# Two orders of their own in the first attention: one for its first step, one for its last

## The chip, the cores and the metric

The kernel runs on one core of a Trainium2 chip. Its engines work side by side and wait for each other through semaphores: TensorE (matmuls), VectorE, ScalarE (called ACT in the profile), GpSimd (POOL) and SyncE (SP), whose queue starts the DMAs here. The metric is the device time of one execution in microseconds (us). The kernel before took 1471.29 us, the median of three runs (1468.84 to 1474.14).

## The reference: what is computed

Two pre-norm transformer layers on `x` of 2 batches x 1024 tokens x 128 channels, in float32. Only the first attention matters here:

```python
q = z @ wq @ fcq_w + fcq_b          # z = layernorm(x); 16 heads of 64
k = z @ wk @ fck_w + fck_b
v = z @ wv @ fcv_w + fcv_b
scores = jnp.einsum('bihd,bjhd->bhij', q, k) / scale
attn = jax.nn.softmax(scores, axis=-1)
out = jnp.einsum('bhij,bjhd->bihd', attn, v)
x = x + (out.reshape(b, n, 1024) @ fco_w + fco_b)
```

It is followed by a mixture of 8 experts with the best 2 chosen per token (its router: a softmax over 8 logits, the two largest, their places), a second attention and a second mixture.

## The kernel before, in words

`l0_attention` works in 16 steps (`STEPS0`): for each of the 2 batches 8 pairs of heads. One step handles 1024 queries against 1024 keys for two heads, in 16 score tiles: 8 blocks of 128 keys (`kt`) times 2 halves of 512 queries (`j`). Softmax needs an upper bound of each row first, so every step also prepares the step behind it.

A step is a list of words (`STEP`), which `step_script` turns into units; every engine runs through the same list and takes its own part of each unit, so the list is the order on every engine:

- `ST`: a score tile. TensorE makes four matmuls into one of three buffers (L933, L934), ACT writes the exponential into `prob` (L680). GpSimd adds the tiles of the eight key blocks for the row sums, two adds of 128x1024 for each block (L623, L628). In the last step GpSimd adds for one head and VectorE for the other (`add_last`, L790).
- `PV`: the product of the probabilities with the values (L906), four matmuls, two units behind the scores (`VALUES_BEHIND`).
- `q`: projections of the next step. TensorE L854, then ACT L638, then VectorE L733.
- `s`: scores of the next step, used for their maxima alone. TensorE L863 and L865, VectorE reduces a tile (L739). There are 16.
- `m`: the maxima turned into a row. TensorE L884, VectorE L744 and L747, then a DMA (`max_rows`, L528) puts the row where the next step's scores read it (`pe.wait_ge(row_loaded, ...)` ahead of `ST` 0).
- `l`: row sums of the step before (TensorE L890, VectorE L751, DMA L536). `r`: their inverse (VectorE L771), sent out and broadcast by DMAs (L541, L544). `n`: the scaling of the output by it (VectorE L775). `g`: output product (TensorE L895, VectorE L779). `r` and `n` have no TensorE part; `g` on TensorE waits for `n`.
- `R`, `X`, `P`: parts of the router for the first batch, in steps 12 and 14, not touched.

`ST`, `q`, `s`, `m`, `l` and `g` share the ring of three score buffers in PSUM (`RING`): a unit may write only when the unit three places before it in the list has been read. An exponential of block `kt` also waits for the value product and the sums of block `kt - 4`, because `prob` has four buffers.

Step 0 has no step behind it whose sums, inverse, scaling and output are due, so `l`, `r`, `n`, `g` and its first two `PV` drop out of the list. The last step has no step to prepare; its list is `LAST_STEP`, and VectorE also does the router's choice for the first batch in it: `probabilities` and `choose_two` after the first sum (L1007 to L1016), when ACT has made the router's exponential (`EXP_AT`, L710), and `index_two` (L1023 to L1029) after the second. Behind the last step stand two value products, the last row sums and the end of the stage.

Of the kernel before, what the change touches and what calls it, by code (L numbers as in the profile page):

```python
# [19 lines left out]
TT = T // P  # L20
# [11 lines left out]
STEPS0 = B * PAIRS  # L32
# [336 lines left out]
def step_units(k_next, k_done):  # L369

    return ([("q", 0), ("q", 1)] * k_next
            + [("s", x) for x in range(S_UNITS)] * k_next + [("m", 0)] * k_next
            + [("l", 0), ("r", 0), ("n", 0), ("g", 0)] * k_done)


STEP = ("ST ST ST ST q q ST PV PV s s s PV PV s s PV ST ST l s s PV X r PV s s s PV PV ST ST ST ST "
        "n ST ST PV s s PV PV s s s PV PV PV s ST ST m g R P PV ST ").split()
LAST_STEP = ("ST ST ST ST PV PV PV PV ST ST ST ST l PV PV PV PV ST ST ST ST PV PV r PV PV ST ST ST ST n "
             "PV PV PV PV g ").split()
VALUES_BEHIND = 2  # L380
TURN_AT, ROOT_AT, NORMAL_AT, LEAD_AT, EXP_AT = 6, 12, (4, 6), 12, 4


STATISTICS_BEHIND = (3, 8)
# [4 lines left out]
def step_script(n):  # L389

    has = step_units(n + 1 < STEPS0, n > 0) + EARLY.get(n, [])
    at = defaultdict(int, PV=-VALUES_BEHIND)
    out = []
    for kind in STEP if n + 1 < STEPS0 else LAST_STEP:
        x = at[kind]
        at[kind] += 1
        if kind in ("ST", "PV"):
            if x >= 0 or n:
                out.append((kind, x // 2, x % 2))
        elif (kind, x) in has:  # L400
            out.append(("UNIT", kind, x))
    return out
# [9 lines left out]
def step_order(n):  # L412

    return [u[1:] for u in step_script(n) if u[0] == "UNIT"]
# [17 lines left out]
def ring_of_pairs():  # L432

    tiles = [("UNIT", u) for u in range(len(in_psum(FIRST_UNITS)))]
    for n in range(STEPS0):
        for what, *rest in step_script(n):
            if what == "ST":
                tiles.append(("ST", 2 * TT * n + 2 * rest[0] + rest[1]))
            elif what == "UNIT" and rest[0] not in "rn":
                tiles.append(("UNIT", place(n, tuple(rest))))  # L440
    return tiles + [("UNIT", first_of(STEPS0))]
# [6 lines left out]
def l0_attention(nc, m, d):  # L448
    with ExitStack() as ctx:
# [182 lines left out]
        def _(act):  # L632
# [24 lines left out]
            for u, (kind, x) in enumerate(in_psum(FIRST_UNITS)):  # L657
                if kind == "q":
                    project(0, x, u)
            for n in range(STEPS0):  # L660
                for what, *rest in step_script(n):
                    if what == "UNIT":
                        if rest[0] == "q":
# [52 lines left out]
        def _(v):  # L716
# [65 lines left out]
            def add_last(kt):  # L782

                v.wait_ge(exp_done, 2 * TT * LAST + 2 * kt + 1 + 1)
                total = psum_k[LAST % 2][:, 1, :]
                if kt == 1:
                    v.wait_ge(filled, place(LAST - 1, ("l", 0)) + 1)
                else:
                    v.wait_ge(last_summed, kt - 1)
                nc.vector.tensor_tensor(total, prob[0][:, 1, :] if kt == 1 else total, prob[kt % 4][:, 1, :],  # L790
                                        ALU.add).then_inc(last_summed, 1)
# [38 lines left out]
            for what, *rest in step_script(LAST):  # L830
                if what == "UNIT":
                    unit(*rest, seen, LAST - 1)
                    seen += rest[0] not in "rn"
                elif what == "ST" and rest[1] and rest[0]:
                    add_last(rest[0])
                    if rest[0] == 1:
                        v.wait_ge(early_act, EXP)
                        probabilities(nc, m, link)
                        choose_two(nc, m, link)
                    if rest[0] == 2:  # L840
                        index_two(nc, m, link)
            run(LAST_UNITS, first_of(STEPS0), LAST, None)

# [160 lines left out]
def probabilities(nc, m, link):  # L1004

    shape = [P, HALF, NEXP]
    link(nc.vector.reduce_sum(m.col[:, 1, :], m.ex[:, :, :], AX.X))  # L1007
    link(nc.vector.reciprocal(m.col[:, 2, :], m.col[:, 1, :]))
    link(nc.vector.tensor_tensor(m.probs[:, :, :], m.ex[:, :, :], m.col[:, 2, :].unsqueeze(2).to_broadcast(shape),
                                 ALU.mult))  # L1010


def choose_two(nc, m, link):

    for t in range(HALF):
        ins = nc.vector.max(m.top[:, t, :], m.probs[:, t, :])  # L1016
    link(ins)


def index_two(nc, m, link):  # L1020

    for t in range(HALF):
        ins = nc.vector.max_index(m.idx[:, t, :], m.top[:, t, :], m.probs[:, t, :])  # L1023
    link(ins)
    nc.vector.tensor_copy(m.idxf[:, :, :], m.idx[:, :, 0:TOPK])
    link(nc.vector.tensor_tensor(m.col[:, 3, :], m.top[:, :, 0], m.top[:, :, 1], ALU.add))
    link(nc.vector.reciprocal(m.col[:, 4, :], m.col[:, 3, :]))
    nc.vector.tensor_tensor(m.col[:, 5, :], m.top[:, :, 0], m.col[:, 4, :], ALU.mult)
    link(nc.vector.tensor_tensor(m.col[:, 6, :], m.top[:, :, 1], m.col[:, 4, :], ALU.mult))  # L1029
# [1693 lines left out]
```

## Time and profile before

| | |
|---|---|
| runs | 1474.14, 1468.84, 1471.29 us |
| profiled execution: own time | 1475.02 us |
| profiled execution: span, first to last instruction | 1473.3 us |
| mean granted TensorE clock | 0.965 |
| first attention, scores of step 0 to the end of its last row sums | 64.8 to 736 us |
| busy VectorE, ACT, GpSimd | 974.1, 810.0, 870.9 us |

The page of the profile gives one execution. A row of its grouped parts is a line of the kernel, the engine, the operation, what it writes and reads, the count, the busy time and the mean duration, and then how long the engine stood idle before these instructions and who ended the idle time. A busy TensorE is not TensorE at its peak: at a granted clock of 0.5 the same matmul takes twice as long and is still busy.

### The profile page before, as it was taken

Reading aid. Unit: us, or ns where it says so; the run is one execution under the profiler, and the core shown is the slowest. Engines: PE = TensorE matmul, PEld = TensorE weight load, DVE = VectorE, ACT = ScalarE, POOL = GpSimd, SP = SyncE. Lnnn points to the kernel's source line nnn. Section 1 sums busy time; section 2 is a strip of 40 time slices with the busy share of each in tenths; the row PEclk is TensorE's granted clock in tenths of the full one; section 3 lists DMA queues with packets and bytes.
Section 4 is the critical chain, followed back from the end, with each engine's and each line's share of the span. In section 5 each row is a group of like instructions: output and inputs, shape, how many; then the busy total and the mean of one; then the engine's idle time right before and its main releaser. Section 6 shows DMA issues by size and latency. Waiting matters only on the chain. (4 is left out here: it accounts for less than half of the span.)

```text
span 1473.3 us, 18699 instructions
## 1 busy us (share of the span) xinstructions
PE 1367.5 (93%) x6354; PEld 791.1 (54%) x6354; DVE 974.1 (66%) x1675; ACT 810.0 (55%) x1236; POOL 870.9 (59%) x685
## 2 busy tenths in 40 slices
PE   7699999999999999999888876999999988999998
PEld 5345555455544555455366633454445446687776
DVE  5676767767776766666556568677666624566665
ACT  4234454454444454354354452566776666787776
POOL 0277888988888888878544405555655232344443
PEclk9699999999999999999999898999999997999999
DMA  3101111111101111000050006011111107000000
GB/s 107 33 1 59 59 59 59 44 59 59 46 28 59 58 59 45 1 16 27 15 160 1 1 1 100 16 30 30 30 22 24 30 1 273 1 1 8 8 8 8
DMA packets 32586, 60.59 MB, mean 41 GB/s; under 512 B 9499, under 2 KB 17084, under 8 KB 32348
## 3 DMA queue, kind: packets, MB, share of 16 engines
q1 hardware_dynamic: 32492, 59.40, 14.6%
q8 instruction: 51, 0.84, 0.2%
q14 instruction: 43, 0.35, 0.1%
HBM read 35.13 MB, written 13.89 MB: 33 GB/s over the span
## 5 line engine op out<-in xcount | busy, mean ns | idle before, releaser
L628 POOL TENSOR_TENSOR psum_k<-psum_k,prob 128x1024 f32<-128x1024 f32 x186 | 466.6, 2541 | 115.4 <-ACT prob L680 114.9
L680 ACT ACTIVATE prob<-pair 128x1024 f32<-128x1024 f32 x256 | 247.7, 1027 | 367.1 <-PE pair L934 366.9
L739 DVE TENSOR_REDUCE mx<-pair 128x2 f32<-128x1024 f32 x256 | 297.2, 1214 | 40.4 <-PE pair L865 38.5
L906 PE MATMUL pv<-prob,c_all 128*64 128x512 f32 x1024 | 251.0, 607 | 0.9 <-ACT plain L648 0.9
L1937 DVE CUSTOM_DVE_ANT_0 l_banks<-l_banks,causal 128x128 f32<-128x128 f32 (+7 forms) x256 | 189.4, 782 | 75.5 <-PE l_banks L1975 74.4
L1845 ACT ACTIVATE l_prob<-l_banks 128x1024 f32<-128x1024 f32 (+7 forms) x256 | 155.2, 654 | 111.7 <-PE l_banks L1994 111.1
L933 PE MATMUL pair<-qq,ak 128*128 128x512 f32 x512 | 210.9, 412 | 6.0 <-issue 2.8
L934 PE MATMUL pair<-q,kb 128*128 128x512 f32 x512 | 203.5, 397 | 0.0
L2153 POOL TENSOR_TENSOR silu_rest_t<-silu_t,silu_lead_t 128x512 fp32r<-128x512 f32 x74 | 96.3, 1303 | 145.9 <-ACT silu_lead_t L2350 145.9
L1899 POOL TENSOR_SCALAR_AFFINE_SELECT l_prob<-l_prob 128x128 f32<-128x128 f32 x256 | 72.3, 295 | 146.7 <-ACT l_prob L1845 145.1
L933 PEld LDWEIGHTS pair<-qq,ak 128*128 128x128 f32 x512 | 97.7, 191 | 70.4 <-issue 29.2
L2519 DVE TENSOR_TENSOR silu_t<-silu_t,bank_t 128x512 f32<-128x512 f32 x128 | 87.9, 688 | 64.4 <-ACT silu_t L2341 60.4
L1975 PE MATMUL l_banks<-l_kk,l_qq 128*128 128x512 f32 (+3 forms) x384 | 114.4, 391 | 14.7 <-DMA l_qq<-rounded 5.2
L906 PEld LDWEIGHTS pv<-prob,c_all 128*64 128x64 f32 x1024 | 61.1, 136 | 119.2 <-issue 110.4
L2341 ACT ACTIVATE silu_t<-bank_t,b_t 128x512 f32<-128x512 f32 x144 | 99.3, 690 | 43.5 <-PE bank_t L953 43.4
L1994 PE MATMUL l_banks<-l_qq,l_kk 128*128 128x512 f32 (+3 forms) x384 | 111.9, 384 | 4.3 <-DVE plain L1937 3.3
L934 PEld LDWEIGHTS pair<-q,kb 128*128 128x128 f32 x512 | 97.8, 191 | 19.3
L863 PE MATMUL pair<-ak,qq 64*128 64x512 f32 x256 | 97.8, 463 | 8.3 <-DVE mx L739 5.3
L1975 PEld LDWEIGHTS l_banks<-l_kk,l_qq 128*128 128x128 f32 x384 | 64.6, 198 | 73.8 <-ACT l_prob L1845 23.5
L863 PEld LDWEIGHTS pair<-ak,qq 64*128 64x128 f32 x256 | 43.7, 189 | 108.0 <-DVE mx L739 40.6
L865 PE MATMUL pair<-kb,qq 64*128 64x512 f32 x256 | 98.0, 463 | 0.0
L1994 PEld LDWEIGHTS l_banks<-l_qq,l_kk 128*128 128x128 f32 x384 | 62.6, 194 | 54.0 <-issue 21.5
(318 smaller groups left out, 2283.0 us busy)
## 6 DMA issues: line engine op xcount, KB each, us to landing
plain<-scratch_sums SPq DMA_DIRECT2D x32, 256.0 KB
whole<-in_experts SPq DMA_DIRECT2D x12, 512.0 KB, 5.0
scratch_lead<-rounded SPq DMA_DIRECT2D x12, 512.0 KB, 2.6
scratch_rest<-rounded SPq DMA_DIRECT2D x12, 512.0 KB, 3.9
w_lead_t<-scratch_lead SPq DMA_DIRECT2D x9, 512.0 KB, 6.4
w_rest_t<-scratch_rest SPq DMA_DIRECT2D x9, 512.0 KB, 7.3
l_kk<-rounded SPq DMA_DIRECT2D x16, 256.0 KB, 4.2
l_qq<-rounded SPq DMA_DIRECT2D x16, 256.0 KB, 5.3
```

The source lines that it names most:

```text
L628: nc.gpsimd.tensor_tensor(total[:, h, :], total[:, h, :], prob[kt % 4][:, h, :], ALU.add).then_inc(summed, 1)
L680: nc.scalar.activation(prob[kt % 4][:, :, ts(j, BLK)], buffer("ST", at)[:, :, :], ACT.Exp, scale=D0 ** -0.5).then_inc(exp_done, 1)
L739: nc.vector.reduce_max(mx[:, x % 2, :, x // 2], buf[:, :, :], AX.X).then_inc(read, 1)
L863: nc.tensor.matmul(buf[:, 0, :], qq[k % 2][0][0:D0, ts(t, P)], m.ak[0:D0, keys], start=True, stop=True)
L906: ins = nc.tensor.matmul(pv[D0 * h:D0 * (h + 1), ts(j, BLK)], m.c_all[:, TT * (s // PAIRS) + kt, :], prob[kt % 4][:, h, ts(j, BLK)], start ...
L933: nc.tensor.matmul(buf, m.ak[:, keys], qq[n % 2][h][:, ts(j, BLK)], start=True, stop=False)
L934: ins = nc.tensor.matmul(buf, m.kb[:, keys], q2[n % 2][:, h, ts(j, BLK)], start=False, stop=True)
L1845: nc.scalar.activation(prob[kt % 2][:, g, P * kt:T], buffer(item)[:, P * kt - T:], ACT.Exp, scale=SCALE1).then_inc(exp_done, 1)
L1937: ins = nc.vector.tensor_tensor_reduce(scores[:, 0:s_width(t)], scores[:, 0:s_width(t)], hidden, 1.0, -3e38, ALU.add, ALU.max, mx[:, g, t: ...
L1975: ins = nc.tensor.matmul(out[:, lo:end], qq[k % 2][:, g, ts(t, P)], kk[k % 2][:, g, lo:end], start=True, stop=True)
L1994: ins = nc.tensor.matmul(buf[:, at:at + end - lo], kk[n % 2][:, g, ts(kt, P)], qq[n % 2][:, g, lo:end], start=True, stop=True)
L2341: nc.scalar.activation(s[n % R][:, :], bank_of(n)[:, :], ACT.Silu, bias=b1[:, c:c + 1]).then_inc(silu_done, 1)
```

## The change

Step 0 gets a list of its own, `FIRST_STEP`, with the same units: `q q` come first, then five `ST`; seven `ST` stand in a row in the middle; after `m` come two `ST` and two `PV`, where one `PV` and one `ST` stood. In `LAST_STEP`, `r` moves from behind `ST` 11 and four `PV` to between `ST` 10 and `ST` 11, `n` from behind `ST` 15 to ahead of `ST` 12, and two `PV` move from ahead of `ST` 12 to behind `ST` 15. ACT makes the router's exponential after score tile 3 instead of 4. `index_two` moves from behind the sum of block 2 to behind the sum of block 7.

```diff
@@ -375,10 +375,12 @@
 STEP = ("ST ST ST ST q q ST PV PV s s s PV PV s s PV ST ST l s s PV X r PV s s s PV PV ST ST ST ST "
         "n ST ST PV s s PV PV s s s PV PV PV s ST ST m g R P PV ST ").split()
-LAST_STEP = ("ST ST ST ST PV PV PV PV ST ST ST ST l PV PV PV PV ST ST ST ST PV PV r PV PV ST ST ST ST n "
+FIRST_STEP = ("PV PV q q ST ST ST ST ST s s PV s s PV PV s s PV ST ST ST ST ST ST ST s PV s s s PV PV PV "
+              "s s s PV PV s s PV PV s s ST ST m ST ST PV PV ").split()
+LAST_STEP = ("ST ST ST ST PV PV PV PV ST ST ST ST l PV PV PV PV ST ST ST r ST PV PV n ST ST ST ST PV PV "
              "PV PV PV PV g ").split()
 VALUES_BEHIND = 2
-TURN_AT, ROOT_AT, NORMAL_AT, LEAD_AT, EXP_AT = 6, 12, (4, 6), 12, 4
+TURN_AT, ROOT_AT, NORMAL_AT, LEAD_AT, EXP_AT = 6, 12, (4, 6), 12, 3
@@ -391,7 +393,7 @@
-    for kind in STEP if n + 1 < STEPS0 else LAST_STEP:
+    for kind in FIRST_STEP if n == 0 else STEP if n + 1 < STEPS0 else LAST_STEP:
@@ -837,7 +839,7 @@
-                    if rest[0] == 2:
+                    if rest[0] == TT - 1:
                         index_two(nc, m, link)
```

## Rows read from the trace of the kernel before

**Rows 1.** Page, busy time, share of the span and instructions of each engine.

```profile
PE 1367.5 (93%) x6354; PEld 791.1 (54%) x6354; DVE 974.1 (66%) x1675; ACT 810.0 (55%) x1236; POOL 870.9 (59%) x685
```

**Rows 2.** Page, costliest groups: adds on GpSimd, exponentials, maxima.

```profile
L628 POOL TENSOR_TENSOR psum_k<-psum_k,prob 128x1024 f32<-128x1024 f32 x186 | 466.6, 2541 | 115.4 <-ACT prob L680 114.9
L680 ACT ACTIVATE prob<-pair 128x1024 f32<-128x1024 f32 x256 | 247.7, 1027 | 367.1 <-PE pair L934 366.9
L739 DVE TENSOR_REDUCE mx<-pair 128x2 f32<-128x1024 f32 x256 | 297.2, 1214 | 40.4 <-PE pair L865 38.5
```

**Rows 3.** Stretches (start:end, length, busy us by engine, clock): step 0, step 2.

```profile
64.83:107.51 42.68, 39.57 (x165) 21.32 (x165) 25.22 (x24) 18.89 (x22) 26.95 (x12) 0.93 0.05 13
149.36:190.50 41.14, 41.14 (x186) 20.82 (x184) 29.95 (x29) 19.44 (x24) 34.66 (x15) 1.00 0.16 53
```

**Rows 4.** Timeline, TensorE, around step 0's start: start, duration, [idle before].

```profile
61.00 1.01 PE L884 MATMUL pair<-ident,mx 128*16 128x128 f32 x4 [2.69 <-DVE mx L739]
64.83 0.77 PE L933 MATMUL pair<-qq,ak 128*128 128x512 f32 x1 [2.82 <-issue]
...
71.29 2.01 PE L854 MATMUL pair<-aq,w_all 128*128 128x512 f32 x8
73.14 0.40 PE L933 MATMUL pair<-qq,ak 128*128 128x512 f32 x1
```

**Rows 5.** Timeline, DMA queue, the row of maxima.

```profile
62.88 0.61 SPq L528 DMA_DIRECT2D q<-mrow  x1
```

**Rows 6.** Stretches at the lower clock: step 0, step 1, last step.

```profile
64.80:70.50 5.70, 5.67 (x13) 4.47 (x14) 0.00 (x0) 2.22 (x3) 0.00 (x0) 0.50 0.32 92
...
108.10:111.30 3.20, 3.20 (x9) 2.48 (x8) 1.60 (x1) 1.58 (x2) 3.20 (x2) 0.52 0.24 96
...
729.00:732.40 3.40, 3.36 (x6) 1.05 (x8) 0.00 (x0) 0.00 (x0) 0.00 (x0) 0.57 0.02 5
```

**Rows 7.** Groups by line, 64.8 to 102.9 us: products for maxima.

```profile
L863 PE MATMUL pair<-ak,qq 64*128 64x512 f32 x16 | 5.9, 446 | 1.3 <-DVE q L733 1.3
```

**Rows 8.** Timeline, TensorE, inside and at the end of step 0.

```profile
76.72 1.94 PE L906 MATMUL pv<-prob,c_all 128*64 128x512 f32 x8
...
102.97 0.61 PE L884 MATMUL pair<-ident,mx 128*16 128x128 f32 x4
...
107.51 0.50 PE L933 MATMUL pair<-qq,ak 128*128 128x512 f32 x1 [1.79 <-DMA q<-mrow]
```

**Rows 9.** Timeline, VectorE, last step.

```profile
704.47 2.98 DVE L790 TENSOR_TENSOR psum_k<-psum_k,prob 128x1024 f32<-128x1024 f32 x1
...
710.35 1.23 DVE L790 TENSOR_TENSOR psum_k<-psum_k,prob 128x1024 f32<-128x1024 f32 x1
711.49 0.68 DVE L751 COPY plain<-pair 128x512 f32<-128x512 f32 x1
...
716.74 0.24 DVE L771 RECIPROCAL plain<-plain 128x16 f32<-128x16 f32 x1
...
725.54 3.35 DVE L775 TENSOR_TENSOR on<-plain 128x1024 f32<-128x1024 f32 x1
...
735.57 0.69 DVE L751 COPY plain<-pair 128x512 f32<-128x512 f32 x1 [1.91 <-PE pair L890]
```

**Rows 10.** Timeline, GpSimd, last step.

```profile
704.00 5.68 POOL L628 TENSOR_TENSOR psum_k<-psum_k,prob 128x1024 f32<-128x1024 f32 x2 [1.38 <-ACT prob L680]
```

**Rows 11.** Timeline, TensorE, last step and the next stage's first product.

```profile
712.23 0.51 PE L933 MATMUL pair<-qq,ak 128*128 128x512 f32 x1 [1.06 <-DVE plain L751]
...
729.04 3.36 PE L895 MATMUL pair<-on,g_all 128*128 128x512 f32 x4 [3.64 <-DVE on L775]
...
737.67 0.47 PE L951 MATMUL h<-rounded 128*128 128x512 f32 x1 [2.17 <-PEq L449]
```

**Rows 12.** Timeline, VectorE, inverse and scaling in step 1.

```profile
128.24 0.25 DVE L771 RECIPROCAL plain<-plain 128x16 f32<-128x16 f32 x1
...
134.62 1.76 DVE L775 TENSOR_TENSOR on<-plain 128x1024 f32<-128x1024 f32 x1 [2.79 <-DMA plain<-scratch_sums]
```

## The prediction

> **What bounds the kernel now.** I read the profile from coarse to fine. The page's first part comes first: TensorE is busy for 93% of the span [rows 1], so it is the engine to free. Next, the stretches of single steps. A step in the steady part of the first attention has TensorE busy for all of its 41.14 us at full clock. The first step takes 42.68 us with 39.57 us busy and a mean granted clock of 0.93 [rows 3], although it does less work (no row sums, no inverse, no output product). So what can be won lies at the two ends of this loop. The waits and the timeline of those ends then say who is late.
>
> At the start, TensorE finishes the maximum products of step 0 at 62.01 us and stands still for 2.82 us until the first score product at 64.83 [rows 4]. What it waits for is the row of maxima, which the DMA queue issues at 62.88 [rows 5]. It then runs at the lower of its two clock levels (1.2 GHz, granted 0.50) until about 70.5 [rows 6]. Inside the step it waits 1.3 us for VectorE's part of the next projections [rows 7]. At the end it waits 1.79 us for the next row of maxima, and the clock falls again from 108.1 to 111.3 [rows 6, 8]. In the last step it stands 1.06 us before VectorE has read the row sums and 3.64 us before VectorE has scaled the output, after which the output product runs at the low level [rows 6, 11]. At both ends the wait that ends last is a wait for VectorE or for the DMA that VectorE starts.
>
> **The first step.** No instruction is added or dropped; the 49 units of the step change places. Durations: the two projection units, eight matmuls, take 1.85 us (71.29 to 73.14 [rows 4]), 0.23 each; at the low level a matmul takes 0.43 (5.7 us for 13 [rows 6]), the pair 3.4. Two value products take 1.94 us [rows 8], of which 0.08 lie beside what follows. A score is four matmuls, 0.92 us. Where the kind of work changes, 0.1 to 0.2 us are added.
>
> Start: the projections of step 1 now stand ahead of the scores. They need neither the maxima nor any buffer that is not yet read, so they run from 61.95 at the low level to about 65.4. The row is there at 64.83, so the scores begin 0.6 us later than before, with 1.85 us of work already done. The clock: it rose 5.7 us after TensorE had begun to work without a pause (64.83 to 70.5) the first time, and 3.85 us after 107.51 the second time. With work from 61.95 on, I take the slower of these, a rise at 67.7. Projections and five scores are 6.64 us at full clock. From 61.95 to 67.7 the low level does 3.1 us of them, the other 3.5 us follow: 71.3. Before, the fifth score ended at 74.07 (73.14 and four matmuls [rows 4]). Gain 2.8 us; with the rise at 65.8 it is 3.6, and with the rise still at 70.5 only 1.5.
>
> Middle: the 1.3 us of [rows 7] go, because VectorE has its share of the projections done by 68, before it has to read a score tile. What is late next are the ring of three score buffers and GpSimd's sums. VectorE reads a tile of maxima in 1.2 us [rows 2]. From 71.3 I laid the new order out block by block with the durations above: seven scores in a row at 77.1, ended at 83.7; maxima s6 to s15 from 83.7 to 94.5. VectorE needs ten reads, 12.1 us, for those and finishes at 96.2, just before the maximum products ask for it at 96.6. Over seven scores in a row an exponential of 1.03 us on ACT [rows 2] falls behind by 0.8 us, which three buffers cover. GpSimd's fourteen sums of 2.5 us [rows 2] then start at 71.5 and their sixth ends at 88.9; the exponential that waits for them comes at 98. The last one ends at 108.3, and the exponential of step 1 that needs it comes at 117. The sum gives the maximum products at 96.6. The same sum over the old order gives 102.5 where the trace has 102.97 [rows 8], so I add 0.3 for small hand-overs: 96.9, a gain of 6.1 us with the shorter queue in front of this point (one score and one value product, 1.8 us, now stand behind it).
>
> End: from the maximum products to the first score of step 1 the path over VectorE and the DMA takes 4.54 us (102.97 to 107.51 [rows 8]). Behind them now stand two scores and two value products, 3.9 us, plus 0.54 for the products themselves: 4.45. The wait of 1.79 shrinks to 0.1. So step 1 begins at 101.4, still 6.1 us early. The low level from 108.1 to 111.3 (granted 0.52 [rows 6]) cost half of its 3.2 us, 1.6. I let it go with the pause that stands ahead of it. First step: 7.7 us.
>
> Here the Trainium skill (TensorE: Matmul & The Clock Gate, What's actually happening) can be read against me: it ties the slow state to an array that is idle, and the fall at 108.1 came only after the array had resumed. Read so, the pause is not its cause and the fall stays: the first step would be worth 6.1 us, not 7.7.
>
> **The last step.** Three VectorE places change: inverse and scaling ahead of the last sums, the index search of the router behind them, and ACT's router exponential one score earlier (0.25 us on ACT ahead of a copy that a value product waits for: up to 0.2 us lost on TensorE).
>
> VectorE's first chain: the wait for that exponential goes, so the second sum starts as soon as its own input is there, at 703.9 instead of 704.47, and the third right behind it instead of behind the index search, which held it until 710.35 [rows 9]. With 2.98 us each the third ends at 709.8 and the row sums are copied by 710.5, not 712.17 [rows 9]. TensorE wants the buffer at 711.2: the 1.06 us [rows 11] go. The sums are then sent off at 710.5. The inverse stands behind the fourth sum, at 713.5 instead of 716.74. A wait is moved with it: the scaling waits for the inverse's DMAs with two sums and the index search queued behind it; only the last row sum product waits for those, at 727.8. From inverse to a released scaling step 1 took 6.4 us [rows 12]: 719.9.
>
> The scaling took 3.35 us here [rows 9] and 1.76 in step 1 [rows 12]; sums take 1.23 alone and 2.98 beside GpSimd [rows 9, 10]. GpSimd's own sums end at 724.3. I take 2.6 for the scaling (722.5), 2.0 and 1.3 for the two sums (725.8). TensorE meanwhile does four scores, two value products, four scores and six value products (3.8 + 1.9 + 3.9 + 5.3 us from 709.3) and reaches the output product at 724.2: the 3.64 us are gone, and with them the low level behind them (0.57 granted over 3.4 us [rows 6], 1.5 us lost). TensorE's side alone gains 1.06 + 3.64 + 1.5 - 0.2 = 6.0 us.
>
> But VectorE now has the index search (2.9 us, 707.45 to 710.35 [rows 9]) behind the last sum: 728.7. Then come the output add, 1.2, and the copy of the row sums, 0.7: 730.7, where the trace has 736.26 [rows 9]. The stage ends 1.4 us after that copy in both (next stage's first product at 737.67 [rows 11]). Gain 5.6 us. Bounds: TensorE's side, 6.0; and with scaling and both sums at their longest (3.35 + 2.98 + 2.98), 2.2.
>
> **Sum.** 7.7 + 5.6 = 13.3 us off the profiled execution: 1475.02 (span 1473.3 and 1.7 around it) to 1461.7. That execution lies 3.7 us above the median 1471.29; the median becomes 1458.0. Nothing behind the attention is changed, and it starts by its own barrier, so I expect no give-back.
>
> **The rivals.**
> 1. *The clock does not follow.* The rise at the start stays at 70.5 (1.3 less), or the fall at step 1 stays (1.6 less). For: at 61.95 to 65.4 the array works after a long stretch at the low level, and the fall at 108.1 came only with the work. And that reading of the Trainium skill's page gives the 1.6. Against: both times that the clock fell here, a pause stood just ahead, and the steady steps have neither. Gain 10.4 with both, 1461.
> 2. *VectorE's tail becomes the bound of the last step.* Scaling and sums beside GpSimd at their longest: 2.2 instead of 5.6, gain 9.9, 1461.4. For: 2.98 us was measured with GpSimd at work. Against: GpSimd runs dry behind each pair of scores. Both rivals together: gain 7.0, 1464.3.
> 3. *Slower.* The new order of step 0 alternates short maxima and value products earlier, while the clock is still low. If the low level held through step 0, each us of it costs 0.47 us. The gain is gone when it lasts 28 us beyond 67.7, to about 96; held to the step's end and once round step 1 (75 us), it costs 35 us, less the 13.3: 1493. Against: in the old step the same alternation, with waits of 1.3 us in it, ran at full clock.
> 4. *The order does not do what it says*: the ring of three makes TensorE wait in the dense parts (s6 to s15 leave VectorE 0.4 us of slack). At one read of 1.2 us lost in each of the eight groups of maxima, 9.6 us go: gain 3.7, 1467.6.
>
> **Chances.** Forecast (gain 11 to 14.5, 1456.8 to 1460.3) 0.70; rival 1 0.12; rival 2 and both together 0.11; rival 4 0.04; rival 3 0.02; 0.01 for what I do not see. What this kernel's measurement can tell from no change is about 0.3%, 4.4 us. The forecast and rivals 1 and 2 are faster by more; rival 4 at its full size falls within. Faster 0.94, within 0.04, slower 0.02. Range: from 1456.8, both ends at their best (8.5 + 6.0), to 1464.3, rivals 1 and 2 together, and 3 us wider below, because the runs before spread by that much around their median: 1453.5 to 1464.5.
>
> **What would show it.** First score of step 0 near 65.4, clock up by 67.8, no TensorE wait for VectorE before s0, maximum products near 96.9, first score of step 1 at 101.4 with a pause under 0.3 us and no low clock. In the last step (all 7.7 earlier): no wait at the tenth score, the output product right behind the value products at full clock, the index search between the last sum and the output add. I am wrong if the border of step 1 keeps a pause over 1 us, if GpSimd's or ACT's waits reach TensorE, or if the middle stage begins less than 10 us earlier.

## The result and the profile after

The changed kernel takes 1462.57 us (median of 7 runs, 1460.86 to 1465.48), the kernel before 1472.87 us in the same comparison (7 runs, 1468.84 to 1475.48). The ratio is 0.9935, 95% interval 0.992 to 0.995: 10.3 us faster by the medians, 7.4 to 11.8 by the interval. The forecast was 13.3, with 11 to 14.5 (1456.8 to 1460.3) as its bounds: 1462.57 lies above them and inside the wider range. The profiled execution took 1465.48 us with a span of 1463.8, 9.5 less than before.

On the page TensorE's busy time is what it was [rows 1]; what fell is the time in which it stands idle:

```profile
PE 1367.6 (93%) x6354; PEld 790.9 (54%) x6354; DVE 977.7 (67%) x1675; ACT 808.8 (55%) x1236; POOL 868.9 (59%) x685
```

The timeline of TensorE in the changed kernel, at the start of step 0, the counterpart of [rows 4] (the kernel has two lines more, so L884 is now L886 and so on; times of this execution are 0.66 us later from the stage before, where nothing was changed):

```profile
61.66 1.01 PE L886 MATMUL pair<-ident,mx 128*16 128x128 f32 x4 [2.69 <-DVE mx L741]
62.61 3.13 PE L856 MATMUL pair<-aq,w_all 128*128 128x512 f32 x8
65.58 0.40 PE L935 MATMUL pair<-qq,ak 128*128 128x512 f32 x1
...
67.02 0.50 PE L935 MATMUL pair<-qq,ak 128*128 128x512 f32 x1 [0.34 <-DVE q L735]
```

The projections stand where 2.82 us of pause were. The clock, in the same stretch as the first of [rows 6], is already up (columns as there; the next to the last two is the granted clock):

```profile
64.80:70.50 5.70, 5.22 (x20) 3.16 (x20) 2.77 (x4) 5.67 (x8) 0.00 (x0) 1.00 0.31 96
```

The end of step 0 on TensorE, the counterpart of [rows 8]:

```profile
97.41 0.61 PE L886 MATMUL pair<-ident,mx 128*16 128x128 f32 x4
...
100.01 1.94 PE L908 MATMUL pv<-prob,c_all 128*64 128x512 f32 x8
102.00 0.50 PE L935 MATMUL pair<-qq,ak 128*128 128x512 f32 x1
```

From the maximum products of step 0 to those of step 1 it is 35.75 us instead of 41.97, and the pause of 1.79 before step 1 has gone.

VectorE in the last step, the counterpart of [rows 9] (copy of the row sums, inverse, scaling, output add, last copy):

```profile
703.51 0.68 DVE L753 COPY plain<-pair 128x512 f32<-128x512 f32 x1
...
706.38 0.24 DVE L773 RECIPROCAL plain<-plain 128x16 f32<-128x16 f32 x1
...
712.58 3.05 DVE L777 TENSOR_TENSOR on<-plain 128x1024 f32<-128x1024 f32 x1 [2.80 <-DMA plain<-scratch_sums]
...
722.21 1.23 DVE L781 TENSOR_TENSOR plain<-pair,plain 128x1024 f32<-128x1024 f32 x1
723.35 0.68 DVE L753 COPY plain<-pair 128x512 f32<-128x512 f32 x1
```

The scaling is done long before TensorE asks for it. TensorE at the end of the step and behind it, the counterpart of [rows 11]:

```profile
717.32 1.98 PE L897 MATMUL pair<-on,g_all 128*128 128x512 f32 x4
...
725.44 0.47 PE L953 MATMUL h<-rounded 128*128 128x512 f32 x1 [3.27 <-PEq L451]
...
730.54 0.79 PE L953 MATMUL h<-rounded,w_lead 128*128 128x512 f32 x1 [1.11 <-DMA w_rest<-scratch_rest]
```

The output product takes 1.98 us instead of 3.36, the wait of 3.64 has gone, and the next stage begins at 725.44 instead of 737.67: 12.2 us earlier. But only 9.5 of them reach the end of this execution. Five us behind the border, from 730.4 on, a low clock appears that the kernel before did not have there:

```profile
729.40:733.80 4.40, 3.29 (x9) 2.58 (x9) 1.38 (x2) 1.21 (x2) 1.89 (x2) 0.62 0.72 195
```

So the question for the experiments: the attention gave what was forecast; what took 2 to 3 us back, and was each term what I said it was?

### The profile page after: what moved, and what is told of

Same layout as the page of the kernel before. It is cut to its first block and busy times, and to the rows that moved or that the text cites. A ratio compares the mean times of both kernels' runs of the same rounds, so it can differ in the third digit from the quotient of the medians.

```text
span 1463.8 us, 18701 instructions
## 1 busy us (share of the span) xinstructions
PE 1367.6 (93%) x6354; PEld 790.9 (54%) x6354; DVE 977.7 (67%) x1675; ACT 808.8 (55%) x1236; POOL 868.9 (59%) x685
## 5 line engine op out<-in xcount | busy, mean ns | idle before, releaser
L935 PEld LDWEIGHTS pair<-qq,ak 128*128 128x128 f32 x512 | 96.0, 188 | 64.8 <-issue 25.6
```

The source lines that it names most:

```text
L935: nc.tensor.matmul(buf, m.ak[:, keys], qq[n % 2][h][:, ts(j, BLK)], start=True, stop=False)
```

## The experiments

Each comparison is with the kernel before, timed on the same chip. Marks read from the timelines of all fourteen profiles are collected here, since the single stages repeat better than the whole execution. "The border" is the first product of the stage behind the attention. (a) from the maximum products of step 0 to those of step 1; (b) from the maximum products of the last step, which step 14 makes, to the border; (c) TensorE's pause at the border; (d) how far behind the border a low clock begins, if one does within 6 us; (e) from the border to the end; (f) how much of (e) the granted clock was at its low level.

```
                 (a)     (b)    (c)    (d)    (e)     (f)
before          41.97   50.74   2.17   no     735.6   63
before again    42.10   51.77   2.17   no     731.5   52
start only      38.19   51.85   2.17   no     731.5   52
first only      36.27   51.92   2.17   no     736.4   67
last only       41.81   45.56   3.3    0.3    735.3   68
after           35.75   45.57   3.27   5.0    738.4   73
after again     35.75   45.56   3.26   0.4    735.4   68
after third     36.31   45.59   3.3    0.0    734.9   68
end undone      38.70   45.57   3.3    0.4    735.4   68
index early     35.74   45.30   2.2    0.7    735.6   68
index mid       35.73   44.47   2.17   no     731.5   55
keep busy       36.30   45.58   0.76   no     734.6   61
index mid busy  36.30   45.12   0.30   no     733.1   55
index mid, four 35.75   44.47   1.0    no     734.8   58
```

The marks repeat to 0.1 us only where the clock in them is the same. With the new step 0 (a) is 35.7 where the clock rises within 3.4 us of the maximum products, and 36.3 where it rises 4.9 us behind them or later. (b) of the old last step is 50.7 in one profile and 51.8 to 51.9 in three. In that one the low clock began 0.4 us after TensorE had resumed and lasted 3.6 us. In the three it began 1.0 to 1.3 us before the end of the pause of 3.64 us and lasted 7 us. The pause in `before_again` ran from 724.5 to 728.1:

```profile
724.50:726.80 2.30, 0.00 (x0) 0.00 (x0) 2.30 (x2) 0.00 (x0) 2.30 (x1) 1.00 0.00 0
726.90:733.70 6.80, 5.60 (x10) 1.86 (x12) 2.28 (x2) 0.00 (x0) 0.00 (x0) 0.50 0.00 0
```

**The first step alone** (`first_only`)

```diff
 # kernel before, plus:
+    for kind in FIRST_STEP if n == 0 else STEP if n + 1 < STEPS0 else LAST_STEP:
```

> The kernel before with FIRST_STEP alone; the last step, the place of the index search and EXP_AT as before. Theory (both ends gain in full and something behind the attention takes 2.7 us back, because TensorE pauses longer there at the border of the stages, 3.27 instead of 2.17 us, and then runs at the lower clock): this kernel keeps the old border, so its whole gain of 7 to 7.7 us reaches the end, 1465 against 1472.5. Rival (the give-back is chance of one execution and has no place in the kernel): the same 7 to 7.7 us here, and the two edits alone add up to the change. Second rival (the first step gains less than the 7.05 us that the trace of after shows): 5 us or less.

Measured: 1466.44 us against 1473.11, ratio 0.9954 (0.9941 to 0.9968): 6.7 us by the medians, 4.7 to 8.7 by the interval. The mark (a) gives 5.7 to 5.8; the border comes 6.4 us earlier, 0.6 of which this execution had ahead of step 0. So the first step's gain is real, it lies inside step 0, and the time shows no part of it lost, though the interval would not show a loss of 1 us.

**The last step alone** (`last_only`)

```diff
 # kernel before, plus the new LAST_STEP, EXP_AT = 3 and
-                    if rest[0] == 2:
+                    if rest[0] == TT - 1:
```

> The kernel before with the last step's order, EXP_AT = 3 and the late index search alone; step 0 as before. Theory (give-back at the border after the last step): the stage ends 5.2 us earlier, but only 2.5 to 3 us arrive at the end, 1469.7 against 1472.5, and the profile shows the low clock behind the stage's first products. Rival (chance of one execution): the full 5.2 us, 1467.3.

Measured: 1468.25 against 1473.11, ratio 0.9967 (0.9953 to 0.9982): 4.9 us by the medians, 2.7 to 6.9 by the interval. That interval holds both numbers, so the time does not decide. The profile does: (b) is 45.56, as in the change to 0.01, and right behind the border, with no first-step edit in it, stands a low clock. It begins 0.3 us behind the border. In `after` it began 5.0 us behind it, directly behind TensorE's wait of 1.11 us for weights; that profile alone could not say which pause it belongs to. The stretch behind the border in this kernel:

```profile
731.10:735.10 4.00, 3.97 (x14) 2.61 (x14) 2.14 (x8) 0.37 (x1) 4.00 (x3) 0.57 0.38 109
```

At 0.57 over 4 us, 1.7 us are lost. The two halves alone add up to 11.6 us by their medians, and the change gives 10.3 us here, 10.1 and 11.1 in the repeats below. The intervals are too wide to call that a difference.

**Both kernels again** (`after_again`, `before_again`), unchanged.

> The changed kernel, unchanged, for a second profile. Theory: start of the next stage near 725 us again, the wait for the weights of expert 1 and the low clock at 731 to 734 come again, ratio 0.9935. Rival: the stretch behind the border differs from the first profile by 2 us or more with nothing changed.

> The kernel before against itself, for a second profile of it and for the size of no change: ratio 1.000 within 0.2%. Theory: no wait of TensorE for the weights of expert 1 and full clock from 738 to 746, as in the first profile. Rival: that stretch differs by 2 us or more with nothing changed.

Measured: 1463.05 us, ratio 0.9942 (0.9923 to 0.996), and 1472.93, ratio 1.000 (0.999 to 1.001). The expectation for `after_again` was partly wrong: the wait for the weights of expert 1 (1.11 us) does not come again in `after_again`. It was chance of one execution, and so are some 2 of the 8.5 us from the border to the second SiLU of that stage, an activation on ACT (6.3 in the repeat). The low clock behind the border does come again, now 0.4 us behind it. The stage behind the border in the kernel before also differs with nothing changed: (e) is 735.6 and 731.5. And the kernel before taught something against my own sum. TensorE at the start of step 1 in `before_again`, and the clock right behind it:

```profile
107.91 0.51 PE L933 MATMUL pair<-qq,ak 128*128 128x512 f32 x1 [1.56 <-DMA q<-mrow]
```

```profile
108.20:111.50 3.30, 3.30 (x16) 2.65 (x16) 2.11 (x1) 2.34 (x3) 3.30 (x2) 1.00 0.11 43
```

The same pause, and no fall: the clock of [rows 6] at 108.1 was not there.

**The end of step 0 as before** (`end_undone`)

```diff
-              "s s s PV PV s s PV PV s s ST ST m ST ST PV PV ").split()
+              "s s s PV PV s s PV PV s s ST ST PV ST m PV ST ").split()
```

> The changed kernel with the end of step 0 as before: score, value, score, maximum products, value, score instead of scores, maximum products, two scores, two values. Theory: the shorter cover behind the maximum products gives back the whole of the old pause, TensorE waits about 1.8 us for the row of maxima; the low clock behind it was chance (it is in the first profile of before and of the last step alone, not in the second profile of before), so with or without it the kernel takes 1.8 us, at most 3.4, more than the change: 1464.5 to 1466. Rival (the pause itself makes the clock fall every time): low level for 3 us or more right behind the pause, 3.4 us more.

Measured: 1463.90 against 1474.12, ratio 0.9943 (0.9922 to 0.9964), the change's time within what can be told apart (0.9935, 0.9942 and 0.9933), and less than the 1464.5 to 1466 that were expected. The profile is clear on the pause. TensorE, first score of step 1, and the clock behind it:

```profile
103.35 0.50 PE L935 MATMUL pair<-qq,ak 128*128 128x512 f32 x1 [1.73 <-DMA q<-mrow]
```

```profile
103.35:107.00 3.65, 3.65 (x16) 3.02 (x17) 0.35 (x1) 2.41 (x3) 3.65 (x2) 1.00 0.71 263
```

The pause is back, to within 0.1 us of the old one; the low clock is not. Over the five executions with this pause (before, before again, start only, last only, end undone) the fall came in two. So the 1.6 us of low clock that I let go with this pause are worth some 0.7 on average, by these five.

**The start alone** (`start_only`)

```diff
 # kernel before, with in step 0:
+FIRST_STEP = ("PV PV q q ST ST ST ST ST s s s PV PV s s PV ST ST s s PV PV s s s PV PV ST ST ST ST "
+              "ST ST PV s s PV PV s s s PV PV PV s ST ST m PV ST ").split()
```

> The kernel before with one edit: in step 0 the two projections stand ahead of the scores; all else in step 0, its end included, and the last step as before. Theory (the first step's gain is 4.1 us at the start, the pause and the slow stretch there plus VectorE's part of the projections, and 1.8 us of pause at the end): maximum products of step 1 about 38 us after those of step 0 instead of 42, the pause of 1.8 us before step 1 still there, 4 us less than before, 1469. Rival (the gain comes from the new middle, seven scores in a row): under 2.5 us.

Measured: 1468.62 against 1473.06, ratio 0.9967 (0.9953 to 0.998): 4.4 us. TensorE at the two ends of the border of step 1:

```profile
98.73 0.61 PE L886 MATMUL pair<-ident,mx 128*16 128x128 f32 x4
...
103.05 0.51 PE L935 MATMUL pair<-qq,ak 128*128 128x512 f32 x1 [1.56 <-DMA q<-mrow]
```

(a) falls by 3.8 to 38.19, and the old pause is still there. The move of two words is worth two thirds of the first step. The remaining 2 us of (a) are the score and the value product that went behind the maximum products, where they fill the old pause; in time that cover was not to be told from nothing (`end_undone`). The seven scores in a row have no gain of their own: `end_undone` has them with the old end and stands at 38.70, this kernel has the old middle with the old end and stands at 38.19, and the later rise of the clock in `end_undone` (5.1 against 3.2 us behind the maximum products) makes up for that difference.

**The index search behind block 5** (`index_mid`), where VectorE stands idle 2.8 us for the DMA of the inverses, instead of in the tail

```diff
-                    if rest[0] == TT - 1:
+                    if rest[0] == 5:
```

> The changed kernel with the index search behind the sum of block 5 instead of block 7, where VectorE stands idle 2.8 us for the DMA of the inverses. Theory (VectorE's tail ends the stage): row sums copied as soon as TensorE has them, stage border 1.0 to 1.2 us earlier (near 724.4), TensorE's pause at the border 2.2 instead of 3.27 us. The clock falls behind the border less often or not at all: 1 to 2.8 us less than the change. Rival (something else ends the stage, or the search beside GpSimd pushes the scaling back): border within 0.3 us of the change's.

Measured: 1461.65 against 1474.12, ratio 0.9924 (0.9906 to 0.9942). VectorE (scaling, last copy of the row sums) and TensorE in this kernel:

```profile
713.77 1.23 DVE L777 TENSOR_TENSOR on<-plain 128x1024 f32<-128x1024 f32 x1
...
721.32 0.69 DVE L753 COPY plain<-pair 128x512 f32<-128x512 f32 x1 [0.57 <-PE pair L892]
```

```profile
723.42 0.47 PE L953 MATMUL h<-rounded 128*128 128x512 f32 x1 [2.17 <-PEq L451]
```

```profile
723.40:728.00 4.60, 3.73 (x19) 2.60 (x20) 2.14 (x8) 1.60 (x4) 4.60 (x3) 1.00 0.44 133
```

Now VectorE waits for TensorE with the last copy, not the other way round: (b) is 44.47, 1.1 us less than in the change, the pause is 2.17, and the clock stays up behind it. The scaling starts 2.1 us later than in the change and takes 1.23 us instead of 3.05, so the sums behind it start only 0.3 us later (measured from the last maximum products). The earlier border shows that in the change VectorE's tail ends the stage, as the prediction said, and that the search was put at the dearer of two places.

**TensorE kept at work** (`keep_busy`): ten matmuls behind the last row sums, whose results nobody reads

```diff
             unit("l", 0, u, LAST)
+            spare = pair[(turn[("UNIT", u)] + 1) % RING]
+            pe.wait_ge(exp_done, 2 * TT * STEPS0)
+            for h in R2:
+                for part in range(5):
+                    nc.tensor.matmul(spare[:, h, :], m.w_all[:, 0, 0, :, :].rearrange("p a c -> p (a c)"),
+                                     m.aq[:, 0:BLK], start=True, stop=True)
```

> The changed kernel with ten matmuls of 512 columns added behind the last row sum product, whose results nobody reads, so that TensorE works for 2.3 of its 3.27 us at the border; VectorE's tail covers them. Theory (the pause at the border, not the weights' DMA, brings the low clock behind it): full clock from the border on, 1.5 us less than the change. Rival 1 (the fall there has nothing to do with the pause): low level for 3.4 us behind the border all the same, time as the change's. Rival 2 (the ten matmuls are not hidden): border up to 2.3 us later.

Measured: 1460.98 against 1474.12, ratio 0.9916 (0.9897 to 0.9935). TensorE at the border, and the stretches behind it (line numbers are higher by the lines added):

```profile
721.53 2.59 PE L947 MATMUL pair<-aq,w_all 128*128 128x512 f32 x10
724.87 0.47 PE L959 MATMUL h<-rounded 128*128 128x512 f32 x1 [0.76 <-PEq L451]
```

```profile
724.80:729.00 4.20, 3.19 (x16) 1.90 (x16) 2.14 (x8) 1.15 (x3) 4.17 (x3) 1.00 0.44 118
729.00:735.00 6.00, 3.98 (x16) 2.72 (x17) 2.46 (x4) 3.44 (x6) 3.04 (x3) 1.00 0.89 261
```

The border stands where it stood (45.58), ten matmuls cost nothing, and the low clock has gone. It is the best median of all, 1.0 to 2.1 us under the three of the change, but the intervals overlap. One thing more goes with it. The low stretch that every profile has some 50 us behind the border, around a pause of 4.3 us, lasts 7 us in all six profiles with a low clock at the border. It lasts 3.5 us in the three with added matmuls and in the four with the old last step. In `after_third` and in this kernel:

```profile
783.50:790.30 6.80, 4.63 (x13) 3.44 (x14) 6.08 (x19) 1.86 (x4) 1.39 (x2) 0.50 0.00 1
```

```profile
779.20:782.60 3.40, 3.40 (x12) 2.24 (x11) 3.30 (x6) 1.39 (x3) 1.04 (x2) 0.51 0.03 7
```

It does not follow the clock at the border alone: `index_mid` has a full clock there and 7 us here.

**Both, and with four matmuls** (`index_mid_busy`, `index_mid_busy4`)

```diff
 # index_mid_busy: the two edits above together; index_mid_busy4:
-                for part in range(5):
+                for part in range(2):
```

> Both together: the index search behind the sum of block 5 and the ten matmuls at the end. VectorE's tail is then 1.1 us shorter than in the change, so the ten matmuls reach to the border itself. Theory: border near 724.4 and no low clock behind it, 2.7 us less than the change. Rival: the matmuls end later than VectorE's copy and hold the stage's end, so border as in the change.

> The index search behind block 5 and four added matmuls instead of ten, so that they end before VectorE's copy of the row sums does (1.0 against 1.9 us). Theory: border as with the search behind block 5 alone (44.5 us after the last maximum products), no low clock behind it, time as that kernel's or up to 1.5 us less. Rival (the clock behind the border does not follow the pause there): low level within 8 us behind the border as in the change.

Measured: 1461.70 against 1474.12, 0.9927 (0.9904 to 0.9949), and 1461.99 against 1473.06, 0.9927 (0.9909 to 0.9944). With ten matmuls (b) is 45.12: they end behind VectorE's shorter tail and hold the stage, as the rival had it, for 0.65 of the 1.1 us that the search had gained. With four it is 44.47. Neither has a low clock within 6 us of the border; the first has one 11 us behind it, 0.7 us behind a pause of 2.31. No gain over either edit alone can be told from these times.

**The index search early** (`index_early`)

```diff
-                    if rest[0] == TT - 1:
+                    if rest[0] == 2:
```

> The changed kernel with the index search back behind the sum of block 2, the inverse and the scaling where the change puts them. Theory (the search only has to stay out of the last stretch; early it holds the row sums back): TensorE waits about 1 us for the copy of the row sums again, the scaling comes as late as the DMA lets it, the border about 1 us later than with the search behind block 5, near the change's. Rival (the scaling's wait for its DMAs is what counts, and it moves by the whole 3 us): TensorE waits 2 us or more for the scaling.

Measured: 1461.76 against 1473.06, 0.9927 (0.991 to 0.9944). TensorE's waits in this kernel's last step (total, times, longest):

```profile
PE h L953 <- PEq L451: 2.2, 1, 2.2
PE pair L935 <- DVE plain L753: 0.9, 1, 0.9
```

The 1 us of [rows 11] before the row sums are read comes back, the scaling is still in time, (b) is 45.30. So the search must stand away from both ends. But this kernel also has a pause of only 2.2 us, as `index_mid`, and a low clock behind it:

```profile
725.20:730.20 5.00, 4.92 (x18) 3.15 (x19) 2.14 (x8) 1.37 (x3) 4.96 (x3) 0.66 0.53 152
```

So a pause of 2.2 us can bring it or not.

**The changed kernel a third time** (`after_third`)

> The changed kernel once more, beside the three above. Theory: pause of 3.3 us at the border and the low clock within 6 us behind it for the fifth time with this tail; ratio 0.993 to 0.9945. Rival: full clock there, then the pause is not what brings it.

Measured: 1461.96 against 1473.06, 0.9933 (0.9915 to 0.995). Pause and low clock came as expected: with a pause of 3.3 us it is five of five (four within 0.4 us of the border, `after` at 5.0), at 2.2 behind a last step at full clock one of two, at 0.3 to 1.0 none of three.

## Why the prediction was right, and where its sum was too large

**Right.** Direction, the wider range, and most of the mechanism. The forecast proper, a gain of 11 to 14.5 us at a chance of 0.70, was not met: 10.3 us lie where rivals 1 (10.4) and 2 (9.9) had their prices, and the timed kernel before stood 1.6 us above the median that the sum started from. That is no hit for these rivals: of rival 1 only the second half came, and of rival 2 the bound but not the price. The range held because it was wide enough for them.

*Start of step 0*: scores at 65.4 were forecast, they came at 65.58 in an execution 0.66 late. The clock rose 3.0 to 6.5 us behind the maximum products, earlier than the 67.7 (6.7 us behind them) that I took, but score tiles then waited 0.34 us for VectorE's projections and for ACT, which I had not in the sum. *Middle*: 35.9 us from maximum products to maximum products were forecast (61.0 to 96.9), 35.75 to 36.3 measured. The forecast was for a late rise, which gives 36.3, so it was 0.4 short and an early rise makes up for it. *End*: pause forecast 0.1, seen 0 (0.4 and 0.6 in two other executions, up to 0.7 with the same step 0 in other kernels). Rival 4, the ring of three, did not show. *Last step*: scaling at 719.9 less 7.1, by which the last maximum products come earlier, is 712.8, seen 712.58; output product right behind the value products at full clock; VectorE's tail as the end; 5.6 forecast, 5.2 seen in (b) against the first profile of before, 6.2 against the three other profiles with the old last step. Luck had a part in that number: the two sums behind the scaling took 4.70 us instead of 3.3, and the index search, no longer beside GpSimd, 2.0 instead of 2.9.

**The step that failed** is the sentence that nothing behind the attention changes and that I expected no give-back, with the term of 1.5 us for the low level at the output product. I counted the pause of 3.64 us and the low clock behind it as gone together. In its place the runs show: the pause in the step goes, but the new tail (index search, output add, copy, all on VectorE) leaves TensorE idle for 3.27 us at the border instead of 2.17. A low clock then comes in the next stage, 1.7 us lost, in five executions of five, and in none of three when TensorE is kept at work there. I had the tail in the working (last row sum product at 727.8, stage end at 732.1) and did not ask what a pause of that length does to the clock.

What that costs in all is less sure. With the pause of 3.3 us the low level takes 68 to 73 us of what lies behind the border, with matmuls in the pause 55 to 61, with the old tail 52 to 67. (e) follows it: 734.9 to 738.4, 733.1 to 734.8, and 731.5 to 736.4. The means of the new and the old tail differ by 2.1 us, but the old tail alone spreads over 4.9, so the size of the give-back is not shown.

**The term that was mis-sized** is the 1.6 us for the fall at 108.1. The first profile of before has it, the second has not; with that pause it came two times in five. One profile of before was too little to write 1.6. Rival 1 named it, at 0.12, and its first half (the rise at the start) did not come true. The reading of the Trainium skill (TensorE: Matmul & The Clock Gate, What's actually happening) that the prediction set against itself, that the pause is not the cause of this fall and that it stays whatever the order, is not borne out: in the nine executions with a covered border of step 1 it never came. It neither follows that pause each time nor comes there without it. Nor does a fall wait for TensorE to resume: three of the four at the old output product began inside the pause.

The account: 13.3 forecast, 12.2 at the border in the first pair of profiles. With the 0.66 by which this execution came late to step 0 they are 12.9: 6.2 in (a), 5.2 in (b), and 1.5 between them, which is the fall at 108.1 of the first profile of before. With 1.7 given back behind the border 12.2 leaves 10.5, where the medians say 10.3, 10.1 and 11.1 (9.6, 8.5 and 9.9 by the ratios). That last agreement is not a proof: (e) alone varies between 731.5 and 736.4 in kernels that do not differ there.

Left open: whether `index_mid` or `keep_busy` really beats the change in time. The traces give 1.1 us at the border to the one and 1.7 us of clock to the other; the timed ratios (0.9924 and 0.9916 against 0.9935, 0.9942 and 0.9933) point that way with overlapping intervals.

## What to carry to other kernels

Work that waits for nothing belongs in front of the first wait of a loop: two words moved gave 4.4 of the 10 us. When a wait is removed, look for where the engine stands idle next, and at which length: the low clock behind the old pause of 3.64 us was followed by one behind the new pause of 3.27. And a term that rests on one clock fall in one profile needs a second profile, while the distance between two marks inside a stage repeated to 0.1 us here where the clock stayed the same, and moved by 0.6 to 1.2 where it did not.

## What the runs showed that I had not expected

A tiny VectorE instruction held that engine for a long time beside GpSimd. At the head of step 14, the small product for the router's normalisation (L822, in the kernel before L820; 128x8, two inputs from SBUF) took 2.0 to 2.3 us in twelve of the fourteen profiles. In the other two it took 11.6. VectorE in `after_again`:

```profile
640.64 2.29 DVE L822 SCALAR_TENSOR_TENSOR plain<-mv,plain 128x8 f32<-128x8 f32 x1
```

and in `after_third`:

```profile
640.49 11.64 DVE L822 SCALAR_TENSOR_TENSOR plain<-mv,plain 128x8 f32<-128x8 f32 x1
```

and GpSimd in `after_third`, a part of its adds, which follow each other without a gap from 623.03 to 652.11:

```profile
635.68 11.81 POOL L630 TENSOR_TENSOR psum_k<-psum_k,prob 128x1024 f32<-128x1024 f32 x5
647.41 4.70 POOL L625 TENSOR_TENSOR psum_k<-prob 128x1024 f32<-128x1024 f32 x2
```

The instruction ended at 652.13, when GpSimd ran dry. In `after_again` GpSimd was as busy, without a gap from 623.18 to 652.28, and the instruction was through after 2.29 us; what decides between the two the runs do not show. TensorE then waited in `after_third` 4.13 us for the projections and ran at the low clock from 653 to 661; from the maximum products of step 1 to those of the last step TensorE took 590.0 us in that execution (588.7 in the other such one) and 582.3 to 584.0 in the twelve without. That is 5 to 8 us more, by chance, in a kernel whose change is worth 10. The Trainium skill (GPSIMD Engine Reference, Key points) says that GpSimd and VectorE contend where VectorE has two inputs from SBUF; the two long cases agree, and show that the wait can last over several of GpSimd's instructions of 2.3 us each.
